# A post-norm attention and FFN kernel on one core: down product by parts of its sum, GpSimd centring four chunks ahead, FFN chunks as straight-line code

## What is computed

```python
for i in range(12):
    qkv = x @ Wqkv[i].T + bqkv[i]
    q, k, v = ...                                   # 16 heads of 8
    att = einsum('bhqd,bhkd->bhqk', q, k) * scale
    y = einsum('bhqk,bhkd->bhqd', att, v)
    x = y @ Wproj[i].T + bproj[i] + x
x = layernorm(x0 + x)
h = silu(x @ wg.T) * (x @ wu.T)                     # wg, wu, wd: integers / 127
x = layernorm(x + h @ wd.T)
```

## Time and profile before

| | |
|---|---|
| median of 3 runs | 326.92 us (326.55 to 327.06) |
| the profiled execution | 327.99 us, span 326.2 us |
| TensorE matmuls busy | 312.0 us, 96% |
| VectorE busy | 227.6 us, 70% |
| ScalarE busy | 182.9 us, 56% |
| GpSimd busy | 96.6 us, 30% |
| chain that ended last | PE 84%, DVE 7%, issue 3%, ACT 2%, POOL 1%, DMA 1% |
| instruction queues | 0.49 MB and 0.07 MB moved |

### The profile page before, as it was taken

How to read it: one execution, slowest core, us unless ns; L and a number is a source line. 1 busy time by engine, 2 the same in 40 slices (tenths; PEclk the granted TensorE clock), 3 DMA queues, 4 the chain that set the end, 5 groups by cost and what they waited for, 6 DMA issues and landing times.

```text
span 326.2 us, 9259 instructions
## 1 busy us (share of the span) xinstructions
PE 312.0 (96%) x3792; PEld 291.6 (89%) x3792; DVE 227.6 (70%) x638; ACT 182.9 (56%) x417; POOL 96.6 (30%) x89
## 2 busy tenths in 40 slices
PE   8999999999999999999999999999999999999992
PEld 8989899898998989989999899898998998888872
DVE  0376877775766757667576775768757669899963
ACT  2448657385574855748557485574851364454530
POOL 2014064140500505005050060410632215565531
PEclk9999999999999999999999999999999999999998
DMA  7832011020010200102001020020000000111112
GB/s 278 325 157 74 6 33 44 2 76 2 18 59 5 74 2 15 65 2 76 2 8 70 4 74 2 2 75 4 1 2 2 3 0 29 35 32 32 34 33 68
DMA packets 7591, 14.90 MB, mean 46 GB/s; under 512 B 512, under 2 KB 4736, under 8 KB 7424
## 3 DMA queue, kind: packets, MB, share of 16 engines
q1 hardware_dynamic: 6976, 13.27, 12.4%
q10 hardware_dynamic: 576, 1.06, 0.9%
HBM read 12.23 MB, written 2.10 MB: 44 GB/s over the span
## 4 chain that ended last, share of the span: by engine, by line
PE 84%; DVE 7%; issue 3%; ACT 2%; POOL 1%; DMA 1%; POOLq 0%; DVEq 0%
PE ps L841 14%; PE ps L788 13%; PE ps L874 13%; PE ps L740 7%; PE ps L738 6%; PE ps L739 6%; PE ps L807 4%; PE ps L953 3%; PE ps L827 3%; PE ps L756 2%; DVE s_rows L572 2%; DVE xt L673 2%; PE ps L942 2%; PE ps L943 2%; PE ps L814 2%
## 5 line engine op out<-in xcount | busy, mean ns | idle before, releaser
L350 POOL TENSOR_TENSOR step_lo<-step,step_hi 128x512 fp32r<-128x512 f32 x44 | 54.8, 1278 | 172.1 <-ACT step_hi L432 172.1
L738 PE MATMUL ps<-state_hi,step_hi 128*128 128x258 f32 x176 | 50.7, 288 | 0.0
L841 PE MATMUL ps<-s_rows,w 32*128 32x256 f32 x768 | 44.8, 380 | 5.3 <-DVE s_rows L572 4.8
L740 PE MATMUL ps<-state_hi,step_lo 128*128 128x258 f32 x176 | 49.9, 283 | 0.0
L739 PE MATMUL ps<-state_lo,step_hi 128*128 128x258 f32 x176 | 49.6, 282 | 0.0
L841 PEld LDWEIGHTS ps<-s_rows,w 32*128 32x128 f32 x768 | 40.4, 185 | 7.3 <-ACT s_rows L426 6.6
L432 ACT CAST step_hi<-step 128x512 fp32r<-128x512 f32 x44 | 27.0, 619 | 33.7 <-DVE step L578 33.7
L788 PE MATMUL ps<-w,gram 128*128 128x128 f32 x352 | 42.8, 275 | 0.0
L788 PEld LDWEIGHTS ps<-w,gram 128*128 128x128 f32 x352 | 42.0, 192 | 0.6
L874 PE MATMUL ps<-step,gram 128*128 128x128 f32 x320 | 40.6, 281 | 0.0
L874 PEld LDWEIGHTS ps<-step,gram 128*128 128x128 f32 x320 | 37.3, 192 | 3.3 <-DVE step L578 3.3
(11 more groups left out here) (102 smaller groups left out, 502.0 us busy)
## 6 DMA issues: line engine op xcount, KB each, us to landing
w<-weights SPq DMA_DIRECT2D x12, 592.5 KB, 3.7
xchan<-x_chan SPq DMA_DIRECT2D x1, 2048.0 KB, 10.6
out<-xchan SPq DMA_DIRECT2D x7, 256.0 KB, 2.3
xt<-x_tok ACTq DMA_DIRECT2D x4, 258.0 KB, 5.4
xt<-x_tok SPq DMA_DIRECT2D x4, 258.0 KB, 4.8
fw_int<-ffn_weights SPq DMA_DIRECT2D x1, 576.0 KB, 4.8
out<-xchan SPq DMA_DIRECT2D x2, 128.0 KB, 3.0
cst<-consts SPq DMA_DIRECT2D x1, 146.5 KB, 7.0
```

Of the source, the lines that this page charges most:

```text
L350: nc.gpsimd.tensor_tensor(group(step_lo, g), group(step, g), group(step_hi_f, g), ALU.subtract).then_inc(step_lo_ready, 1)
L738: nc.tensor.matmul(dst, l_hi, r_hi, start=True, stop=False)
L740: return nc.tensor.matmul(dst, l_lo, r_hi, start=False, stop=True)
L841: last = nc.tensor.matmul(n_banks(h)[:, k, :], w[r, s, WQ + P * i:WQ + P * (i + 1)], s_rows[r, h, i, :], start=i == 0, stop=i == QUADS - 1)
```

## The change

Three edits, all in the FFN part.

The down product's two loops change places: j (the hidden part) is now outside and t (the token tile) inside. The waits for hid 0, 1 and 2 stand at the head of their four products. All four sums of a bank are open at once, and the flag that starts a sum is set only on the first product into each bank.

GpSimd's `centre` stands behind `norm2` instead of ahead of rstd2, and works for chunk c + 4 instead of c + 3. It waits for the z product of chunk c + 2. The centre of chunk 3 is done ahead of the first chunk.

The loops over chunks go on SP, GpSimd, ScalarE, VectorE and, in the branch that is taken, on TensorE. The same functions are called eight times with constants.

```diff
--- before.py
+++ after.py
@@ -308,7 +308,7 @@
                 sp.wait_ge(n_done, 2 * k + 2)
                 sp.wait_ge(shift_ready, k + 1)
                 sp.dma_start(w[:, k % 2, :], weights[k + 2]).then_inc(w_in[k % 2], 16)
-            with loop(sp, CHUNKS - 1) as c:
+            for c in range(CHUNKS - 1):
                 sp.wait_ge(o_ready, c + 2)
                 sp.dma_start(out_v[bass.ds(c, 1), :, :, :].rearrange("a p t c -> (a p) t c"),
                              o[:, bass.ds(c * (CT * P), CT * P)].rearrange("p (t c) -> p t c", t=CT)).then_inc(out_done, 16)
@@ -376,16 +376,16 @@
                     o[:, bass.ds(n * (CT * P), CT * P)].rearrange("p (t c) -> p t c", t=CT), y[:, :, :],
                     rstd2[:, :].unsqueeze(2).to_broadcast([P, CT, P]), ALU.mult).then_inc(o_ready, 1)
 
-            def chunk(c, slot, ahead=3):
+            def chunk(c, slot, ahead=4):
 
                 if ahead >= 2:
                     pool.wait_ge(h1_ready, (c + 1) * CT + CT)
                     rstd1_part(c + 2)
-                if ahead >= 3:
-                    pool.wait_ge(z_done, c + 2)
-                    centre(c + 3, 1 - slot)
                 if ahead > 0:
                     norm2(c)
+                if ahead >= 4:
+                    pool.wait_ge(z_done, c + 3)
+                    centre(c + 4, slot)
 
             pool.wait_ge(o_ready, 1)
             rstd1_part(0)
@@ -393,10 +393,9 @@
             centre(2, 0)
             pool.wait_ge(h1_ready, CT)
             rstd1_part(1)
-            with loop(pool, CHUNKS // 2 - 2) as i:
-                for s in range(2):
-                    chunk(i * 2 + s, s)
-            for c in range(CHUNKS - 4, CHUNKS):
+            pool.wait_ge(z_done, 2)
+            centre(3, 1)
+            for c in range(CHUNKS):
                 chunk(c, c % 2, CHUNKS - 1 - c)
             for h in range(2):
                 pool.wait_ge(ve2_ready, CHUNKS + h)
@@ -494,11 +493,8 @@
             nub_copy(2)
             ht_copy(0)
             nub_copy(3)
-            with loop(act, CHUNKS // 2 - 1) as i:
-                for s in range(2):
-                    chunk(i * 2 + s, s)
-            chunk(CHUNKS - 2, 0)
-            chunk(CHUNKS - 1, 1, last=True)
+            for c in range(CHUNKS):
+                chunk(c, c % 2, last=c == CHUNKS - 1)
 
 
         @block.vector
@@ -706,11 +702,8 @@
 
             dve.wait_ge(nub_ready, GROUPS)
             nc.vector.memset(var2[:, :], 0.0).then_inc(y_ready, 1)
-            with loop(dve, CHUNKS // 2 - 1) as i:
-                for s in range(2):
-                    chunk(i * 2 + s, s)
-            chunk(CHUNKS - 2, 0, ahead=1)
-            chunk(CHUNKS - 1, 1, ahead=0)
+            for c in range(CHUNKS):
+                chunk(c, c % 2, CHUNKS - 1 - c)
 
             last_slot, parts = 1, [range(CT)[part] for part in halves]
             for h in range(2):
@@ -945,15 +938,16 @@
 
             def down_stage(n, last_chunk=False):
                 pe.wait_ge(y_ready, n + 1)
-                for t in range(CT):
-                    for j in range(HC):
-                        if t == 0:
-                            pe.wait_ge(hid_ready, n * HC + (HC + j + 1))
+
+                first, final = ((0, CT // 2), (CT // 2 - 1, CT - 1)) if last_chunk else ((0,), (CT - 1,))
+                for j in range(HC):
+                    pe.wait_ge(hid_ready, n * HC + (HC + j + 1))
+                    for t in range(CT):
                         bank = HT_BANK if last_chunk and t >= CT // 2 else DOWN_BANK
                         last = nc.tensor.matmul(ps[:, bank, P * t:P * (t + 1)], hid[:, j, P * t:P * (t + 1)],
-                                                wd[:, j, :], start=j == 0, stop=j == HC - 1)
-                    if last_chunk and t == CT // 2 - 1:
-                        last.then_inc(down_done, 1)
+                                                wd[:, j, :], start=j == 0 and t in first, stop=j == HC - 1 and t in final)
+                        if last_chunk and j == HC - 1 and t == CT // 2 - 1:
+                            last.then_inc(down_done, 1)
                 last.then_inc(down_done, 1)
 
             a_stage(0)
@@ -990,11 +984,12 @@
                 down_stage(c, last_chunk=ahead == 0)
 
             def chunks(low):
-                with loop(pe, CHUNKS // 2 - 1) as i:
-                    for s in range(2):
-                        chunk(i * 2 + s, s, low)
-                chunk(CHUNKS - 2, 0, low, ahead=1)
-                chunk(CHUNKS - 1, 1, low, ahead=0)
+                if low:
+                    with loop(pe, CHUNKS // 2 - 1) as i:
+                        for s in range(2):
+                            chunk(i * 2 + s, s, low)
+                for c in range(CHUNKS - 2 if low else 0, CHUNKS):
+                    chunk(c, c % 2, low, CHUNKS - 1 - c)
```

## The result

The changed kernel took 323.0 us in the median of its first four executions (322.45 to 324.19), the kernel before 326.9. The ratio is 0.9873, with a 95% interval of 0.9834 to 0.9912. Two more measurements of the same program gave 0.9886 (0.9860 to 0.9913) and 0.9869 (0.9834 to 0.9904). Over all three the changed kernel's 15 executions have a median of 323.1 us, and 49 executions of the kernel before, taken beside all runs of this document, one of 326.9. Two more executions of the kernel before, of 394.6 us at a granted clock of 0.756 and of 331.5 us at 0.990, were slow and are in no figure here.

The account below looks back on a forecast made before the run. TensorE was taken as the floor at 6.84 us per chunk, kept waiting by late VectorE work. Gains of 2.52 (chunks 1 to 5) and 0.80 (chunk 6) sum to 3.32 us: 323.6 us from the median 326.92, range 323.0 to 325.6.

Parts of the forecast that it names:

- the blocked square: VectorE's square of y beside GpSimd's centre: 1.12 us instead of 0.29, 0.83 lost in each of chunks 1 to 5.
- the centre clears the squares of z: GpSimd's moved centre ends by 5.55 us into a chunk, 0.22 us before VectorE's squares of z start.
- the first half's y: Last chunk: y of the first half starts at 5.41 us after the chunk's start, where it was 5.20.
- the tail: Work after the last chunk's down product: gain 0, the second half's y at 6.58 us at the latest, before 6.54.
- straight code: Chunk loops written out: code fetch taken as 0; rival of 0.7 us per chunk gives 329.2 us, chance 0.05.
- The 2.52: Chunks 1 to 5: with the centre moved they take 6.84 us each, 34.20 instead of 36.72, gaining 2.52 us.
- The 0.80: Chunk 6: the down product by parts removes its stalls, 5.95 us instead of 6.75, gaining 0.80 us.
- the lower end: Bottom of the forecast range, 323.0 us: forecast less 0.6, from a run 0.37 under the median and 0.2 for the tail.
- the 7.18 us: Time of chunks without a loop turn, put on late VectorE; rival that it stays: 325.3 us, chance 0.14.
- its ring of 6.74: Steps through three engines that make the next chunk's h1, 6.74 us, 0.10 below TensorE's 6.84.
- the second rival's price: Centre meets the squares of z in chunks 1 to 4: 2.92 us lost, 326.5 us, chance 0.08.
- the bound for code fetch: Upper limit for fetching the longer code: 0.7 us per chunk, the longest weight-load gap that no releaser explains.

Follow-up runs that it names:

- again: The changed kernel, unchanged, measured once more; 323.3 us in the median of 5 executions.
- again_two: The changed kernel, unchanged, measured a further time; 322.8 us in the median of 6 executions.
- centre_back: The changed kernel with GpSimd's centre back between its two powers, three chunks ahead; 323.5 us, ratio to the kernel before 0.9876.
- before_again: The kernel before, unchanged, run for one more trace; 327.4 us in 1 execution.
- write_beside: The changed kernel plus a GpSimd memset of a 128x512 tile that nothing reads, where the centre stood before; 322.7 us in 1 execution.
- centre_twice: The changed kernel plus a copy of the centre into an unread tile, ahead of each of four centres; 323.9 us, ratio to the kernel before 0.990.

## Why the prediction was right or wrong

**Right.** TensorE is the floor in every chunk; the blocked square makes VectorE late; the centre clears the squares of z, by 0.29 to 0.31 us where 0.22 was forecast; the first half's y comes 0.2 us later and the tail does not change by more than 0.06; straight code costs nothing that shows. The split of the gain holds as well: the centre alone gave 2.77 us (forecast 2.52), and the order by parts on top of it 0.72 (forecast 0.80).

**Wrong: the size.** The terms of the sum were small by a little. The 2.52 took its period from chunk 0 as 6.84 us; it was 6.81 to 6.82, and the term measured 2.65. The 0.80 measured 0.83, and chunk 0 gave 0.01 where nothing was put. The tail gave 0.06 us where I had 0. With them the forecast is 3.55 us, 323.4 us, which still lies in the range. The measured difference of the medians, 3.8 us over all executions, lies 0.2 us above, and the first measurement, 4.2 us by its ratio, 0.6. Both lie within what the parts outside the FFN vary; that all of the rest is such variation isn't shown.

**Wrong: the range.** The step that failed is the lower end, the forecast less 0.6. It took 0.37 us from three executions of before that lay within 0.5 us and 0.2 for the tail, and had nothing for what single executions vary outside the FFN. The 49 executions of before go from 325.8 to 330.5 us, the changed kernel's fifteen from 322.2 to 324.6, and from the last VectorE instruction to the end of the span alone the traces of these two kernels differ by 1.2 us. Half a microsecond more room below would have held the result. The side on which it came out is partly luck: the ratio of again gives 323.2 us, inside the range, that of again_two 322.6, outside.

**Wrong, without effect on the number: what the 7.18 us were.** The prediction said that VectorE is late and named no ring that has the block in it: its ring of 6.74 does not pass through the squares of y. The ring that closes is y, hidden parts, the rest of the down product, y. Either of two edits opens it: the centre takes 0.83 us out, the order by parts 0.75 (7.10 to the 6.35 through hid 0). VectorE's own round was missing too, 6.88 us with the block and 7.26 with the loop's turns. Asked what is late next, the prediction looked at neither. That both lie below TensorE once the centre has moved, 7.10 - 0.83 = 6.27 and 6.05 us by estimate, was luck as far as the prediction goes. Hence centre_back is only 0.36 us slower, and for a period of 7.18 us with all three edits no run shows a ground. The edits' gains alone, 2.77, 1.53 and 1.31, sum to 5.6 us, and together they give 3.49.

**Wrong: the second rival's price**, 2.92 us. Forced, it cost 0.56. The price let the ring grow by the full block, as if the centre moved with the squares.

**Wrong, without effect: the bound for code fetch.** The 0.66 us before L841 that no releaser explains stand where the last layer waits for s_rows: in before_again the loads there show 0.60 us of idle time with ScalarE's s_rows as releaser. It is a wait in the code and bounds no fetch.

## What to carry to other kernels

Before pricing an edit, close every ring that passes through the stage that waits, with both engines' steps in it, and see how many of the planned edits cut the same ring: their gains do not add. A consumer that needs its inputs later (here the sum ordered by its parts) can open such a ring as well as a producer that is earlier. Where the expected gain is about 1%, read it from a stretch of the trace that repeats (here within 0.02 us), and take the range's width from what varies outside it.

## What the runs showed of the hardware

A VectorE square with both inputs in SBUF is blocked for the whole rest of a GpSimd instruction that reads 128x512 values from SBUF and ends 0.14 or 0.15 us after it (1.12 us instead of 0.29 in before), but not by a memset of the same size (write_beside), nor by a GpSimd power of 128x4 values, which lasts 1.02 us and also reads SBUF: in centre_twice two squares wholly inside one kept their 0.29 us. The GpSimd instruction itself loses little: 1.04 to 1.19 us with the collision, 1.04 without.

Four sums kept open at once in one bank, each left after every product, cost nothing: the 24 weight loads take 2.76 us in either order.

A turn of a loop costs VectorE about 0.4 us, and TensorE nothing that shows.
